# Second expert products with the tokens as the standing side, in a kernel of mixture of experts, attention and mixture of experts

## The reference

```
dispatch = einsum('sec,sd->ecd', sec_mask, tokens)      # 320 token rows per expert
h = gelu(einsum('ecd,edf->ecf', dispatch, w1))          # 320 x 512
expert_out = einsum('ecf,efd->ecd', h, w2)              # 320 x 128
out = einsum('sec,ecd->sd', combine_weights, expert_out)
```

## Time and profile before

| what | value |
|---|---|
| time of 3 executions | median 545.29 us, 543.77 to 549.74 |
| the profiled execution's own time | 548.49 us |
| its span, from first to last instruction | 546.7 us |
| mean granted TensorE clock | 0.971 of full |
| PE busy | 460.0 us, 84% of the span |
| VectorE, ScalarE, GpSimd busy | 52%, 46%, 41% |
| first experts stage | about 69 to 161 us |
| second experts stage | about 445 to 536 us |

### The profile page before, as it was taken

One profiled execution on the slowest core, in us unless ns is written; L12 is line 12 of the kernel. 1 busy time (PEld: TensorE's weight loads), 2 busy tenths in 40 slices (PEclk: granted clock), 3 DMA queues, 4 the chain that ended last, 5 costly groups with the idle time before them and its releaser, 6 DMA issues.

```text
span 546.7 us, 10834 instructions
## 1 busy us (share of the span) xinstructions
PE 460.0 (84%) x3148; PEld 301.2 (55%) x3153; DVE 282.1 (52%) x1526; ACT 249.3 (46%) x563; POOL 223.8 (41%) x289
## 2 busy tenths in 40 slices
PE   3456099999958889999999999999999679999990
PEld 2345057666633555666565666665655327766660
DVE  4764332333222766577868685868583522343221
ACT  4444124434411555575666666564646304444430
POOL 5576501534562535150535334441214510335455
PEclk9999999999988899999999999999999889999995
DMA  8833135555432440000000010000001122554520
GB/s 296 222 120 125 42 88 150 155 160 169 122 111 73 140 153 2 1 20 2 22 16 26 12 32 11 24 18 19 23 12 37 41 63 82 156 165 141 169 91 29
DMA packets 46496, 45.67 MB, mean 84 GB/s; under 512 B 6859, under 2 KB 35684, under 8 KB 46416
## 3 DMA queue, kind: packets, MB, share of 16 engines
q1 hardware_dynamic: 41840, 36.87, 22.3%
q0 software_dynamic: 4608, 8.22, 4.5%
HBM read 29.35 MB, written 19.17 MB: 89 GB/s over the span
## 4 chain that ended last, share of the span: by engine, by line
PE 46%; DVE 6%; issue 4%; POOL 2%; ACT 2%; DMA 2%; POOLq 0%; SPq 0%; DVEq 0%; ACTq 0%
PE sc L715 9%; PE sc L604 6%; PE sc L708 5%; PE b L779 5%; PE b L614 4%; DVE junk L1334 3%; PE sc L722 3%; POOL out L1561 2%; PE b L760 2%; PE b L789 2%; PE b L593 2%; ACT probs L1040 1%; PE b L683 1%; PE b L558 1%; PE b L698 1%
## 5 line engine op out<-in xcount | busy, mean ns | idle before, releaser
L1334 DVE CUSTOM_DVE_ANT_0 junk<-sc,cht 128x256 bf16<-128x256 f32 (+1 forms) x256 | 84.8, 387 | 52.4 <-PE sc L715 52.3
L1541 POOL DMA_INDIRECT slots<-pay,slot_i x64 | 63.6, 994 | 40.1 <-issue 15.8
L975 ACT ACTIVATE hT<-sc 128x320 f32<-128x320 f32 x128 | 55.7, 437 | 52.0 <-PE sc L604 38.8
L604 PE MATMUL sc<-enT,w1s 128*128 128x320 f32 x256 | 76.1, 442 | 0.8 <-DMA w1s<-in_L_ffn_w 0.5
L614 PE MATMUL b<-hT,w2s 128*128 128x320 f32 x256 | 73.8, 432 | 0.0
L1040 ACT ACTIVATE probs<-sc 128x1024 f32<-128x1024 f32 x48 | 49.2, 1026 | 53.2 <-PE sc L722 52.4
L715 PE MATMUL sc<-qkT 32*128 32x256 f32 (+1 forms) x512 | 66.1, 376 | 0.0
L722 PE MATMUL sc<-qnT,qkT 32*128 32x256 f32 x448 | 65.6, 404 | 0.0
L1561 POOL DMA_INDIRECT x<-yrow,ytok x40 | 39.0, 974 | 60.1 <-DVE yrow L1303 49.5
L1561 POOL DMA_INDIRECT out<-yrow,ytok x40 | 38.9, 974 | 59.4 <-DVE yrow L1303 48.5
L604 PEld LDWEIGHTS sc<-enT,w1s 128*128 128x128 f32 x256 | 48.3, 193 | 22.1 <-issue 4.5
(11 more groups left out here) (147 smaller groups left out, 791.3 us busy)
## 6 DMA issues: line engine op xcount, KB each, us to landing
w1s<-in_L_ffn_w SPq DMA_DIRECT2D x32, 256.0 KB
w2s<-in_L_ffn_w SPq DMA_DIRECT2D x32, 256.0 KB
slots<-fresh SPq DMA_DIRECT2D x16, 330.0 KB, 5.2
rows<-slots SPq DMA_DIRECT2D x16, 330.0 KB
xall<-in_L_attn_x SPq DMA_DIRECT2D x8, 256.0 KB
xall<-x SPq DMA_DIRECT2D x8, 256.0 KB, 2.8
out<-xall SPq DMA_DIRECT2D x8, 256.0 KB
slots<-pay,slot_i POOLq DMA_INDIRECT x64
```

Source lines behind the costliest of these rows:

```text
L604: mm(hid[f], w1s[a][:, P * f:P * (f + 1)], enT[:, :, HALF * a:HALF * (a + 1)], start=True, stop=True).then_inc(e_hid, 1)
L975: nc.scalar.activation(hT[a][:, f, :], hid[f], ACT.Gelu_apprx_tanh).then_inc(e_gelu, 1)
L1334: ins = v.tensor_tensor_reduce(junk[:, head, lo:], sc[h][:, jj, 2 * P * g + lo:2 * P * (g + 1)], table[:, lo:], scale=1.0, scalar=MASKED, ...
L1541: gp.indirect_dma_start(out=slots_d[phase], out_offset=bass.IndirectOffsetOnAxis(ap=slot_i[s][:, t:t + 1], axis=0), in_=pay[s][:, t, :], i ...
```

## The change

The second products are made with the tokens as the standing side. For each slice f and each chunk c, 64 tokens of expert a stand (`hT[a][:, f, 64 c : 64 c + 64]`, 128 x 64) and w2's slice f of expert a streams (128 columns). The result goes to partitions 64 a to 64 a + 63 of bank b6 (chunks 0 to 3) or b7 (chunk 4), which is already token order. Both experts of the pair are made in one function `down(p)`, with a innermost, so that neighbouring products use the two halves of TensorE's columns. There are 4 x 5 x 2 = 40 products of 128 x 64 standing and 128 streaming. `y_copy` on ACT and `turn_back` on PE are gone with their semaphores, and `add_back` reads b6 and b7. One semaphore `e_down` stands for both experts.

With it the orders change. PE's step p is `up(p, 0)`, `up(p, 1)`, `turn_in(p+1)`, `down(p)`. DVE's is `copy_in(p+1)`, `norm(p+2)`, `add_back(p)`. SP's list stays, with both waits for `e_yps` now waits for `e_down`.

```diff
# SP
-                        sp.wait_ge(e_yps[1], g)
+                        sp.wait_ge(e_down, g)
                         sp.dma_start(w2s[1][:], w2_e[bass.ds(p * 2 + 1, 1)].rearrange("e p c d -> (e p) c d")).then_inc(w2_in[1], 16)
...
-                    sp.wait_ge(e_yps[0], g + 1)
+                    sp.wait_ge(e_down, g + 1)
                     sp.dma_start(w2s[0][:], w2_e[bass.ds(nxt, 1)].rearrange("e p c d -> (e p) c d")).then_inc(w2_in[0], 16)
# PE
                 def turn_in(p):
                     g = p + g0
-                    wait(pe, e_rows, (max(g - 2, g0) if isinstance(p, int) else g - 2) * PC)
+                    wait(pe, e_xT, g)
...
-                def down(p, a):
-                    g = p + g0
-                    pe.wait_ge(w2_in[a], (g + 1) * 16)
-                    wait(pe, e_yT[a], g)
-                    for f in range(FC):
-                        pe.wait_ge(e_gelu, (g * 2 + a) * FC + f + 1)
-                        last = mm(yps[a], w2s[a][:, f, :], hT[a][:, f, :], start=(f == 0), stop=(f == FC - 1))
-                    last.then_inc(e_yps[a], 1)
-                def turn_back(p):
...
+                def down(p):
+                    g = p + g0
                     for a in range(2):
+                        pe.wait_ge(w2_in[a], (g + 1) * 16)
+                    wait(pe, e_rows, g * PC)
+                    for f in range(FC):
+                        pe.wait_ge(e_gelu, (g * 2 + 1) * FC + f + 1)
+                        for c in range(PC):
+                            for a in range(2):
+                                y = b6[:, P * c:P * (c + 1)] if c < 4 else b7[:, 0:P]
+                                last = mm(y[HALF * a:HALF * (a + 1)], hT[a][:, f, HALF * c:HALF * (c + 1)], w2s[a][:, f, :],
+                                          start=(f == 0 and c in (0, 4)), stop=(f == FC - 1), skip_group_check=True)
+                    last.then_inc(e_down, 1)
                 def step(p):
                     if has(p, PAIRS):
                         up(p, 0)
-                    if has(p - 1, PAIRS):
-                        down(p - 1, 1)
-                    if has(p, PAIRS):
                         up(p, 1)
                     if has(p + 1, PAIRS):
                         turn_in(p + 1)
...
-                        turn_back(p - 1)
                     if has(p, PAIRS):
-                        down(p, 0)
-                    if has(p - 1, PAIRS) and not (isinstance(p, int) and p == PAIRS - 1):
-                        turn_back(p - 1)
+                        down(p)
# ACT
-                    wait(act, e_yps[a], g)
+                    wait(act, e_down, g)
                     for f in range(FC):
                         act.wait_ge(e_hid, (g * 2 + a) * FC + f + 1)
                         nc.scalar.activation(hT[a][:, f, :], hid[f], ACT.Gelu_apprx_tanh).then_inc(e_gelu, 1)
-                def y_copy(p, a):
...
                 def step(p):
+                    gelus(p, 0)
+                    gelus(p, 1)
# DVE
                     v.tensor_copy(ytok[u][:, :], r[:, :, TOKEN])
-                    dve.wait_ge(e_back, g + 1)
+                    dve.wait_ge(e_down, g + 1)
                     for c in range(PC):
-                        v.scalar_tensor_tensor(yrow[u][:, c, :], b4[:, P * c:P * (c + 1)] if c < 4 else b5[:, 0:P],
+                        v.scalar_tensor_tensor(yrow[u][:, c, :], b6[:, P * c:P * (c + 1)] if c < 4 else b7[:, 0:P],
                                                r[:, c, WEIGHT:WEIGHT + 1], r[:, c, 0:D], ALU.mult, ALU.add).then_inc(e_rows, 1)
                 def step(p, j, u):
                     if has(p + 1, PAIRS):
-                        norm(p + 1)
                         copy_in(p + 1)
-                    if has(p - 1, PAIRS):
-                        add_back(p - 1, (u + 1) % 2, j + (u - 1) + g0 // 2)
-                sweep2(dve, step, -1, E2_LO, E2_HI, PAIRS + 1)
+                    if has(p + 2, PAIRS):
+                        norm(p + 2)
+                    if has(p, PAIRS):
+                        add_back(p, u, j + g0 // 2)
+                norm(0)
+                sweep2(dve, step, -1, E2_LO, E2_HI, PAIRS)
```

More of the change, by code:

```diff
@@ L228, in macaron @@
         hT = [sb(f"hT{i}", [P, FC, CAP]) for i in range(2)]
-        yT = sb("yT", [P, PC, P])
         yrow = [sb(f"yrow{i}", [P, PC, D]) for i in range(2)]
@@ L270, in macaron @@
         hid = [sc[0][:, 0, 0:CAP], sc[0][:, 1, 0:CAP], sc[1][:, 0, 0:CAP], sc[1][:, 1, 0:CAP]]
-        yps = [b6[:, 0:CAP], b7[:, 0:CAP]]
         b7r, b7s, b7v = b7[:, D:2 * D], b7[:, 2 * D:2 * D + H * SINKS], b7[:, 3 * D:4 * D]
@@ L314, in macaron @@
         e_gelu = sem("e_gelu")
-        e_yps = [sem("e_yps0"), sem("e_yps1")]
-        e_yT = [sem("e_yT0"), sem("e_yT1")]
-        e_back = sem("e_back")
+        e_down = sem("e_down")
         e_rows = sem("e_rows")
@@ L502, in experts @@
                 if phase == 0:
-                    sp.wait_ge(e_yps[1], PAIRS)
+                    sp.wait_ge(e_down, PAIRS)
                     sp.dma_start(w2s[1][:], w2_e[1]).then_inc(w2_in[1], 16)
@@ L642, in step @@
                             warm(3)
-                    elif has(p, PAIRS):
-                        turn_back(p - 1)
                     if has(p, PAIRS):
-                        down(p, 0)
-                    if has(p - 1, PAIRS) and not (isinstance(p, int) and p == PAIRS - 1):
-                        turn_back(p - 1)
+                        down(p)
                 pe.wait_ge(scattered[PAYS - 1], 16 * TB * (B // PAYS) * (1 + phase))
                 warm(8)
-                sweep(pe, step, -1, E_LO, E_HI, PAIRS + 1)
+                sweep(pe, step, -1, E_LO, E_HI, PAIRS)
             bank4.drain(pe, 0)
@@ L664, in _ @@
             pe.wait_ge(e_rows, PAIRS * PC)
-            for a in range(2):
-                pe.wait_ge(e_yT[a], PAIRS)
             pe.wait_ge(weights_in, 16 * N_WEIGHTS)
@@ L975, in gelus @@
                         nc.scalar.activation(hT[a][:, f, :], hid[f], ACT.Gelu_apprx_tanh).then_inc(e_gelu, 1)
-                def y_copy(p, a):
[L978 to L982, removed]
-                def step(p):
-                    if has(p, PAIRS):
-                        gelus(p, 0)
-                    if has(p - 1, PAIRS):
[L988 to L993, removed]
+                def step(p):
+                    gelus(p, 0)
+                    gelus(p, 1)
+                sweep(act, step, 0, E_LO, E_HI, PAIRS)
             experts(0)
```

## The result

| | before | after |
|---|---|---|
| median, range | 546.96 us, 543.77 to 549.74 (4 runs) | 608.85 us, 608.58 to 610.78 (4 runs) |
| profiled execution: span, clock | 546.7 us, 0.971 | 607.2 us, 0.960 |

The ratio is 1.114, with a 95% interval of 1.107 to 1.122. The forecast was 578 us, 560 to 587: slower was right, but the change costs 62 us and not 33.

A forecast was written before the change was run, and what follows sets the result against it. TensorE was taken to bound the kernel, setting each experts pair's 10.4 us. The new wait for add_back (+18.3 us) and falls of the clock (+15 us) summed to 33 us, giving 578 us, range 560 to 587.

The forecast's parts named there:

- w2s and the rows behind e_down: Sign on SP: w2s[0] and the rows are issued just behind the end of both experts' second products.
- norm released by the rows and yrow behind it: Sign on VectorE: the rows' landing releases norm 12 times; add_back's yrow line follows, ending 7.65 us after down(p).
- TensorE released by yrow twelve times: Sign on TensorE: down(p+1) waits for add_back, six times a phase, making pairs 12.3 us against 10.4, +18.3 us together.
- ScalarE's 13.6 us: Sign on ScalarE: it is busy less by its yT copies, 13.6 us.
- rival C: Second products: column halves don't run side by side, down takes 8.6 us instead of 4.3, total 632 us; chance 0.05.
- down(p) is then 4.6 us from its start to e_down: Second products on TensorE: 4.3 us for 80 records, plus 0.15 for entering and 0.17 for the last record's tail.
- POOL scatters from about +6.6: POOL after down(p) ends: five scatters of 1.28 us each, needed by VectorE only two pairs later.
- The gap: TensorE between second products: down(p+1) can start 7.7 us after down(p) ends, held by add_back behind norm.
- Rival D: w2s[1] behind the rows slows their landing by up to 0.8 us: 573 us, at most 586; chance 0.08 with few falls.
- The clock: TensorE's clock falls after the new wait, costing 0 to 1.7 us a pair; 1.5 us in 10 of 12 pairs, 15 us.
- Rival A: Experts stages: the wait but no or few falls of the clock, +18 us, 563.5 us; chance 0.2.
- Rival B: TensorE remains the bound if rows land 1.9 us after e_down: pair 9.5 us against 10.4, 533 us; chance 0.04.

The follow-up runs named there:

- e9: The changed kernel once more, without an edit, in a later job with stops: 606.41 us, ratio 1.113 to the kernel before.
- e11: Changed kernel, with POOL holding the scatters of pairs 0 to 5 until the next pair's second products are made: 605.01 us, ratio 1.111 to the kernel before.
- e7: Changed kernel with rows issued two pairs ahead, TensorE's steps written out, w2 in two buffer sets loaded a pair ahead; job without stops: 527.61 us, ratio 0.988.
- e2: Changed kernel with SP issuing the rows two pairs ahead instead of one: 553.45 us, ratio 1.018 to the kernel before.
- e4: Changed kernel with the rows two pairs ahead and TensorE's steps written out instead of a loop: 552.1 us, ratio 1.017 to the kernel before.
- e14: Kernel before, plus 80 unread small bf16 products a pair ahead of expert 0's second products, where the last scatter ends: 603.65 us, ratio 1.109.
- e1: Changed kernel with VectorE doing add_back(p) ahead of norm(p+2): 559.92 us, ratio 1.027 to the kernel before.
- e12: The same kernel as e7, in a job with stops: 549.81 us, ratio 1.009 to the kernel before.
- e15: Changed kernel with add_back ahead of norm and scatters held until turn_in(p+2), beside the next second products; job with stops: 600.51 us, ratio 1.103.
- e5: The same edit to the changed kernel as e11, in a job without stops: 591.36 us, ratio 1.105 to the kernel before.
- e8: e7's kernel with scatters up to pair 5 held until three quarters of the next second products are made; job without stops: 534.25 us, ratio 1.000.
- e17: e7's kernel with scatters up to pair 6 held until three quarters of the next second products are made; job without stops: 538.36 us, ratio 1.008.
- e18: e7's kernel again, without any hold of the scatters, beside e17 in a job without stops: 528.48 us, ratio 0.989.

## Why the prediction was right and wrong

Right, by its own steps: w2s and the rows behind e_down; norm released by the rows and yrow behind it; TensorE released by yrow twelve times; ScalarE's 13.6 us. So are column halves side by side: down(0) takes 4.51 us from start to start where 4.3 and 0.15 were forecast, so rival C (8.6 us) is out.

The step that failed is "down(p) is then 4.6 us from its start to e_down". I took the price of 80 records from rows in which nothing else went on, and used it for twelve places where POOL scatters beside them. Today that can't be seen, since a second product is eight records and no row of the experts stages has a run of more than 16 (a sign outside them, on VectorE, is in the last section). My sentence on the scatters ("POOL scatters from about +6.6 ... and VectorE needs that only two pairs later") asked only who waits for them. With the measured values in the forecast's sum, for the profiled execution:

- down(1) to down(6): 12 x (7.73 - 4.6) = +37.6 us. e9 against e11 shows that they come with the scatters.
- down(7), which has scatters too: 5.9 and 5.8 us, +2.5 us.
- The gap: 7.95 us in the mean (between the windows above, from 7.0 to 8.7) against 7.7, 12 x 0.25 = +3.0 us. The rows land later, 3.6 us after issue in the pair shown and 4.2 us in the one that starts at 114.59. Rival D had the place right (up to 0.8 us a pair).
- The clock: 15 us forecast for falls in ten pairs. It fell in six, over five second products and one set of first products, and next to nothing was paid for it, since down takes its 7.7 us at either level and the first products had the wait behind them: -15 us.

33.3 + 37.6 + 2.5 + 3.0 - 15 = 61.4 us; the span grew by 60.5.

So the clock's mechanism was there but rarer than forecast, and the stops hid its cost. e11 has it in the open: twelve falls, 12 x 1.87 = 22 us, more than the 1.5 us in ten pairs that I took. The end of 1.7 us was too low: the low stretch can be longer than the 3.4 us of rows 8 (at a mean of 0.60, the 7.53 us from 105.00 hold 6.0 us at 1.2 GHz). A rule of the Trainium skill stood beside this ("TensorE: Matmul & The Clock Gate", Part 4: turns don't hold the clock up), and e11's windows agree with it: five turns in each gap kept the clock up in none of twelve. In the changed kernel the same five turns stood in the gaps and the clock was full over seven of the twelve second products, so the turns alone don't decide it.

Rival A, the wait alone with its 18 us, was seen in no run. Rival B, the pair of 9.5 us, had its pair priced right, and "if the rows land 1.9 us after e_down" was the right question; e7 meets its condition and has 9.57 us a pair, though it needed w2 ahead as well, and gains 5.9 us where 12.6 were priced.

## What to carry to other kernels

A price per instruction taken from a short run, or from a quiet stretch, does not hold for a long run of short ones: when a change turns 8 long records into 80 short ones, look at what runs beside them, GpSimd's scatters first, and price the long run in that place. When a moved wait makes an engine idle, ask which other work it pushes on top of the next burst; here a swap of two steps on VectorE put the scatters into the idle time and gave back 48 of 62 us. And two costs on one stretch need not add: in e11 the stops of twelve second products went, the clock fell over all twelve and down(7) got their scatters, and the time stayed the same.

## What the hardware showed that I had not expected

- Runs of short TensorE records stop for 0.2 to 1.4 us beside GpSimd's scatters, with nothing that the profile names; the later pieces start 0.72 us apart or at a multiple. How many records pass before the first stop differs: 52 to 70 in down(1) to down(6) of the changed kernel, 47 and 50 in its down(7), 33 to 42 in down(1) to down(6) of e2 and e4, 27 to 30 in ten pairs of e14. That looks like a store of instructions that empties, and a supply behind it that scatters slow down, but this is only argued: no row shows TensorE's instruction supply, and no run tells GpSimd's issuing of a scatter from the transfer that it starts. The Trainium skill ("TensorE: Matmul & The Clock Gate", Back-to-back issue gap) tells of a 64-deep reorder window through which weight loads and products go, which is of this order of size; no run here shows that it is the store in question.
- The stops aren't always there: in two of five jobs none, in no kernel. The kernel before was faster by 2% in those jobs as well. What differs I can't tell; the first job (stops) and the second (none) have the same chip number on record. The changed kernel itself never ran in a job without stops, so what the change costs there isn't measured.
- With 64 standing columns and fp32, records of two column halves run side by side at the full rate: 80 records in 4.51 us, 0.056 us each.
- It isn't TensorE alone. In routing, beside GpSimd's scatters into the slot table, VectorE stands still too. Lines of the timeline of the kernel before, of a job with stops:

```profile
50.73 0.32 PE L569 MATMUL b<-onehot,cht 128*128 128x64 bf16 x4
...
55.13 0.23 DVE L1222 TENSOR_TENSOR place<-b,base 128x64 f32<-128x64 f32 x1 [4.44 <-remote]
```

and of the same two steps in e7, of a job without:

```profile
49.59 0.32 PE L569 MATMUL b<-onehot,cht 128*128 128x64 bf16 x4
...
49.95 0.23 DVE L1192 TENSOR_TENSOR place<-b,base 128x64 f32<-128x64 f32 x1 [0.82 <-PE b L569]
```

The step waits for the product alone, which ended at 51.05 and at 49.91. In six profiles of jobs with stops (before, after, e1, e9, e12, e15) VectorE idles for 4.0 to 5.7 us at this step or the next one of its kind, in those of e5 to e8, e17 and e18 at neither. e12, the same kernel as e7, idles for 5.70 us here, and its first second products begin 4.4 us later than e7's (79.91 against 75.47), before any of the changed work. So part of what differs between the two kinds of job lies outside the experts stages, and the trace of the kernel before had a sign of it that the forecast didn't use.
